# Router tail, threshold search and first expert lists of a GNN and mixture-of-experts kernel, rebuilt

## The reference

```python
x = x + _L1_gnn_ref(_layernorm(x), src, dst, ...)
# _L1_ffn_ref, on _layernorm(x):
capacity = max(1, int(Sz * CAP_FACTOR / E) + 1)          # 1250 * 2 / 8 + 1 = 313
scores = softmax(einsum('bsd,ed->bse', x, router_w))     # 8 experts
gate_vals, sel_idx = top_k(scores_t, capacity)           # 313 tokens for each expert
tokens = x[b_idx, sel_idx]
h = gelu(einsum('becd,edh->bech', tokens, w1) + b1)
y = einsum('bech,ehd->becd', h, w2) + b2
out = zeros_like(x).at[b_idx, sel_idx].add(y * gate_vals[..., None])
```

## Time and profile before

| | |
|---|---|
| median of 3 runs | 1624.05 us (1623.88 to 1624.58) |
| profiled execution | 1622.14 us, its span 1620.5 us |
| PE busy | 1487.8 us, 92% |
| DVE busy | 926.6 us, 57% |
| ACT / POOL busy | 592.5 / 351.0 us |
| mean granted TensorE clock | 0.963 of full |

### The profile page before, as it was taken

One profiled execution on the slowest core, in us unless ns is written; L12 is line 12 of the kernel. 1 busy time (PEld: TensorE's weight loads), 2 busy tenths in 40 slices (PEclk: granted clock), 3 DMA queues, 4 the chain that ended last, 5 costly groups with the idle time before them and its releaser, 6 DMA issues.

```text
span 1620.5 us, 30075 instructions
## 1 busy us (share of the span) xinstructions
PE 1487.8 (92%) x9025; PEld 801.8 (49%) x9025; DVE 926.6 (57%) x2130; ACT 592.5 (37%) x814; POOL 351.0 (22%) x300
## 2 busy tenths in 40 slices
PE   7887899999999999989999999999999728999996
PEld 5443454545455454434454444444545426667664
DVE  7886888686978887451432232223275565566542
ACT  4686647373535544220112220001122204465541
POOL 3222211202201110360800003500023201432232
PEclk9898899999999999999999999999999857999998
DMA  6000000000352433331301113420133335778753
GB/s 247 21 27 14 8 27 26 13 13 26 98 169 94 155 130 115 133 116 66 117 0 36 42 52 117 155 91 1 53 125 122 116 125 169 211 215 247 218 143 48
DMA packets 55682, 158.13 MB, mean 98 GB/s; under 512 B 6980, under 2 KB 8467, under 8 KB 55608
## 3 DMA queue, kind: packets, MB, share of 16 engines
q1 hardware_dynamic: 43704, 115.57, 19.9%
q0 software_dynamic: 11904, 41.62, 10.3%
HBM read 115.39 MB, written 41.78 MB: 97 GB/s over the span
## 4 chain that ended last, share of the span: by engine, by line
PE 72%; DVE 12%; issue 10%; ACT 3%; POOL 1%; DVEq 1%; DMA 1%; ACTq 0%; SPq 0%; POOLq 0%
PE ps L1219 25%; PE ps L1290 11%; PE ps L1414 8%; PE ps L1398 7%; PE ps L1130 3%; PE ps L1131 3%; PE ps L1132 3%; PE ps L1054 2%; PE ps L584 2%; PE ps L1386 1%; PE ps L1084 1%; DVE hm L1827 1%; DVE bstat L538 1%; ACT th L1484 1%; PE ps L1369 1%
## 5 line engine op out<-in xcount | busy, mean ns | idle before, releaser
L1219 PE MATMUL ps<-wa,tb 128*128 128x512 f16 x960 | 210.1, 379 | 3.7 <-DVEq L2176 1.6
L1290 PE MATMUL ps<-adj,nm 128*128 128x512 f16 (+1 forms) x960 | 178.6, 345 | 2.9 <-DVEq L2158 1.6
L1130 PE MATMUL ps<-gp,hop 128*128 (+1 forms) x400 | 152.8, 382 | 7.2 <-issue 3.7
L1131 PE MATMUL ps<-gp,hop 128*128 (+1 forms) x400 | 152.6, 382 | 0.0
L1132 PE MATMUL ps<-gp,hop 128*128 (+1 forms) x400 | 152.6, 382 | 0.0
L1219 PEld LDWEIGHTS ps<-wa,tb 128*128 (+1 forms) x960 | 92.9, 98 | 113.3 <-issue 4.3
L1290 PEld LDWEIGHTS ps<-adj,nm 128*128 x960 | 93.4, 97 | 88.5 <-issue 4.1
L1414 PE MATMUL ps<-wa,hT 128*105 128x512 f16 x576 | 126.8, 379 | 1.7 <-issue 1.7
L1591 ACT ACTIVATE tb<-cx 128x512 f32 (+1 forms) x48 | 26.8, 559 | 268.4 <-DVE cx L2148 268.4
L1219 PE MATMUL ps<-wb,hop 128*128 128x512 f16 x480 | 108.8, 388 | 0.0
L1398 PE MATMUL ps<-tkT,wb 128*128 128x315 f16 x768 | 107.2, 301 | 1.1 <-ACT tkT L1640 1.1
(11 more groups left out here) (361 smaller groups left out, 2372.1 us busy)
## 6 DMA issues: line engine op xcount, KB each, us to landing
w_st<-in_ew SPq DMA_DIRECT2D x16, 2048.0 KB, 10.5
self_d<-cr SPq DMA_DIRECT2D x20, 512.0 KB, 2.9
cr<-self_d SPq DMA_DIRECT2D x20, 512.0 KB, 4.3
stage<-in_wn POOLq DMA_DIRECT2D x16, 512.0 KB, 4.0
x_d<-cr SPq DMA_DIRECT2D x10, 512.0 KB, 4.5
cx<-x_d SPq DMA_DIRECT2D x10, 512.0 KB, 4.6
cr<-x_d SPq DMA_DIRECT2D x10, 512.0 KB, 4.3
out<-cr SPq DMA_DIRECT2D x10, 512.0 KB, 2.7
```

Of the source, the lines that this page charges most:

```text
L1130: pe.matmul(acc, wh, gh, start=(s_ == 0), stop=False, skip_group_check=True)
L1131: pe.matmul(acc, wh, gl, start=False, stop=False, skip_group_check=True)
L1219: ins = pe.matmul(ps[:, b + c, :], lhs(part, k), w[:, w_, k, c * 512:(c + 1) * 512], start=(k == 0 and part == 0 and w_ == 0), stop=(last ...
L1290: ins = pe.matmul(ps[:, 6 + j, 0:w_], nm[:, part, s_, bass.ds(f * P, P)], adj[:, s_, CC * c:CC * c + w_], start=(s_ == 0 and part == 0), s ...
```

## The change

`chained` takes a `tail`: the loop stops one turn earlier, and the last tiles are written out on each engine. There TensorE runs route(3, 1) before the transposes of tile 8, and route(4, 0) right behind them; ScalarE copies both parts of tile 8; the low part of tile 9 is made on VectorE, not on GpSimd; tile 9's three router products add up in one PSUM region, the maximum and the exponential read it there, and the mask of the padding rows (`live`) is folded into the last two operations.

In the search the ten rounds are unrolled on VectorE and TensorE. The number of cuts found is summed as integer powers of two straight into new bits (`found`), the next cuts are `base | found`, and `base` is made while TensorE counts. The compare is two instructions of five tiles each, and TensorE starts with the first. Constants are written early, in `first_low`.

For experts 0 and 1 TensorE waits for each one-hot tile by itself (tile outside, chunk inside). `s_idx` is signalled by the operation that writes `idx`. Each gathered chunk has its own semaphore, and TensorE waits for one chunk at a time, for all eight experts.

```diff
+def chained(loop, steps, tail, per=0, early=None):
...
-    with loop(1, NT // 2, per) as r:
+    with loop(1, NT // 2 - 1, per) as r:
         at(r, 0), at(r, 1)
-    at(NT // 2, 0, NT), at(NT // 2, 1, NT + 1)
+    at(NT // 2 - 1, 0)
+    tail()
...
-            with g.Fori(0, NT // 2) as r:
+            def full_d(i, j):
+                t = 2 * i + j
+                g.wait_ge(D_.aff, D_.r + t + 1)
+                g.sem_inc(s_tick, 1)
+                g.wait_ge(D_.lo, D_.m + t)
+                g.sem_inc(s_tick, 1)
+                g.tensor_scalar(cy[:, 0, :], cr[:, j, :], lnv[:, 1, j:j + 1], lnv[:, 2, j:j + 1],
+                                ALU.mult, ALU.add).then_inc(D_.y, 1)
+
...
+                g.wait_ge(D_.y, D_.n + 2 * i + j + 1)
+                g.sem_inc(s_tick, 1)
+                ln_low(g, D_, i, j, cy, dyh[:, j, 0, :], dyh[:, j, 1, :])
+
+            with g.Fori(0, NT // 2 - 1) as r:
...
-
-            g.wait_ge(s_live, 1)
+                    full_d(r, j), low_d(r, j)
+            full_d(NT // 2 - 1, 0), low_d(NT // 2 - 1, 0), full_d(NT // 2 - 1, 1)
...
+                if isinstance(t, int) and t == NT - 1:
+                    for k in range(KT):
+                        for n, (part, w_) in enumerate(((0, 0), (0, 1), (1, 0))):
+                            ins = pe.matmul(ps[:, 6 + j, 0:8], dyT[:, j, part, k, :], rws[:, k, 8 * w_:8 * w_ + 8],
+                                            start=(k == 0 and n == 0), stop=(k == KT - 1 and n == 2))
+                    ins.then_inc(D_.mm, 1)
...
+            def tail():
+                last = NT // 2 - 1
+                neighbours(1, last, 1), route(last - 1, 1)
+                turn_d(last, 0), route(last, 0)
+                turn_d(last, 1), route(last, 1)
+
...
-            with pe.Fori(0, BITS // STEP) as b:
-                pe.wait_ge(s_cm, b + 1)
+            for b in range(BITS // STEP):
                 for t in range(NT):
+                    if t % 5 == 0:
+                        pe.wait_ge(s_cm, 2 * b + t // 5 + 1)
                     ins = pe.matmul(ps[0:TP, 6, 0:CUTS * NE], ones16[0:TP, 0:TP], at_least[:, t].rearrange("p m n -> p (m n)"),
                                     start=(t == 0), stop=(t == NT - 1))
                 ins.then_inc(s_cnt, 1)
...
+                if isinstance(e, int) and e < 2:
+                    for t in range(NT):
+                        pe.wait_ge(s_sel0, NT * e + t + 1)
+                        for c in range(3):
+                            ins = pe.matmul(ps[0:SLOT, 0, 4 * c:4 * c + 4], selm[:, t, c * SLOT:(c + 1) * SLOT], tokg[:, t, e, :],
+                                            start=(t == 0 and c == 0), stop=(t == NT - 1), skip_group_check=True)
+                    ins.then_inc(s_lst, 1)
+                    return
...
-                pe.wait_ge(s_gx[j], 48 * (i + 1))
                 for c in range(3):
+                    pe.wait_ge(s_gx[j][c], 16 * (i + 1))
...
+            def tail():
+                last = NT // 2 - 1
+                evac_d(last, 0), evac_d(last, 0, 1)
+                ln_d(last, 1)
+                route(last - 1, 1), route(last, 0)
+                evac_d(last, 1), route(last, 1)
+
             chained(lambda a_, b_, _: s.Fori(a_, b_), [
...
+            def logits(i, j):
+                t = 2 * i + j
+                v.wait_ge(D_.mm, t + 1)
+                if isinstance(t, int) and t == NT - 1:
...
+                    link(v.tensor_reduce(col(j, 16), ps[0:TP, 6 + j, 0:8], AX_X, ALU.max))
+                else:
+                    link(v.tensor_copy(rtmp[:, j, 0:8], ps[0:TP, 6 + j, 8:16]))
+                    link(v.tensor_tensor(rtmp[:, j, 8:16], ps[0:TP, 6 + j, 0:8], rtmp[:, j, 0:8], ALU.add))
...
+            def scores(i, j):
+                t = 2 * i + j
+                v.wait_ge(s_dex, t + 1)
...
+                if isinstance(t, int) and t == NT - 1:
+                    link(v.tensor_scalar(col(j, 20), col(j, 19), live[:, 0:1], None, ALU.mult))
+                    v.tensor_scalar(sc[:, t, :], rtmp[:, j, 24:32], col(j, 20), live[:, 1:2], ALU.mult, ALU.add).then_inc(s_sc, 1)
+                else:
+                    v.tensor_scalar(tile_of(sc, t), rtmp[:, j, 24:32], col(j, 19), None, ALU.mult).then_inc(s_sc, 1)
...
+            def tail():
+                last = NT // 2 - 1
+                out_c(last, 1), stats_d(last, 1)
+                logits(last - 1, 1), logits(last, 0)
+                v.wait_ge(D_.y, D_.n + NT)
+                ln_low(v, D_, last, 1, cy, dyh[:, 1, 0, :], dyh[:, 1, 1, :])
+                scores(last - 1, 1), scores(last, 0)
+                evac_d(last, 1), route(last, 1)
+
+            chained(step.loop, [(out_c, 0), (stats_d, 0), (evac_d, 1), (route, 2)], tail, 2 * (1 + LINKS + 3), early=first_low)
 
...
+            found = thr[:, 1, :]
+            for b in range(BITS // STEP):
+                shift = BITS - STEP * (b + 1)
+                if b:
+                    link(v.tensor_tensor(cuts[:], base[:], per_cut(found), ALU.bitwise_or))
+                now = cuts if b else bits
+                for h in range(2):
+                    v.tensor_tensor(at_least[:, 5 * h:5 * h + 5], sc[:, 5 * h:5 * h + 5].unsqueeze(2).to_broadcast([TP, 5, CUTS, NE]),
+                                    now[:].bitcast(F32).unsqueeze(1).to_broadcast([TP, 5, CUTS, NE]), ALU.is_ge).then_inc(s_cm, 1)
+                if b < BITS // STEP - 1:
+                    if b:
+                        link(v.tensor_tensor(thr[:, 0, :], thr[:, 0, :], found, ALU.bitwise_or))
...
+                    v.wait_ge(s_cm, 2 * b + 2)
+                    link(v.tensor_scalar(bits[:], bits[:], 0.5 ** STEP, None, ALU.mult))
+                    link(v.tensor_tensor(base[:], per_cut(thr[:, 0, :]), bits[:], ALU.bitwise_or))
+                else:
+                    link(v.tensor_tensor(thr[:, 0, :], thr[:, 0, :], found, ALU.bitwise_or))
                 v.wait_ge(s_cnt, b + 1)
-                link(v.tensor_scalar(over[:], counts, float(CAP), None, ALU.is_ge))
-                link(v.tensor_reduce(nd[:, 0, :], over[:].rearrange("p m n -> p n m"), AX_X, ALU.add))
-                link(v.tensor_tensor(thr[:, 1, :], nd[:, 0, :], low_bit[:], ALU.mult))
-                link(v.tensor_tensor(thr[:, 0, :], thr[:, 0, :], thr[:, 1, :], ALU.bitwise_or))
+                link(v.tensor_scalar(over[:], counts, float(CAP), float(1 << shift), ALU.is_ge, ALU.mult))
+                with nc.allow_low_precision(reason="at most seven equal powers of two: exact as integers"):
+                    link(v.tensor_reduce(found, over[:].rearrange("p m n -> p n m"), AX_X, ALU.add))
+            link(v.tensor_tensor(thr[:, 0, :], thr[:, 0, :], found, ALU.bitwise_or))
...
+                    if isinstance(e, int) and e < 2:
+                        ins.then_inc(s_sel0, 1)
+                if not (isinstance(e, int) and e < 2):
+                    ins.then_inc(s_sel, 1)
...
+                v.tensor_tensor(idx[:, j, :], lst[:, j, :, 0], pads[:], ALU.add).then_inc(s_idx, 1)
...
-                v.sem_inc(s_idx, 1)
...
```

89 lines of the change are left out of this document (35 added, 54 removed).

## The result

| | median of the runs, us | ratio to before, 95% interval |
|---|---|---|
| before, in the same job | 1624.32 (1623.88 to 1625.63, 4 runs) | |
| after | 1609.96 (1607.34 to 1611.39, 4 runs) | 0.9909 [0.9893, 0.9924] |
| after, unedited, in a later job | 1607.27 (1605.83 to 1609.04, 4 runs) | 0.9894 [0.9879, 0.9908] |

The change saves 14.4 us in the first job and 16.9 in the later one, where before had a median of 1624.18; 15.7 was forecast. The profiled execution of after took 1611.06 us, its span 1609.4.

A forecast was written before the change was run, and what follows sets the result against it. In the search no engine is full; a serial chain from router tail to gathers delays the expert stage. 2.7 + 7.8 + 2.1 + 0.5 + 2.9 - 0.3 = 15.7 us; 1624.05 - 15.7 = 1608.4 us, range 1605.5 to 1611.8.

The forecast's parts named there:

- Tail: Router's last tiles: reordering, VectorE's subtraction and the shorter softmax start the first compare 2.7 us earlier, bounds 1.9 to 3.7.
- Search: Ten search rounds: 2.23 us per round in place of 3.02, gaining 7.8 us, bounds 5.4 to 8.6.
- the ring with its slower price: Second rival, search: each half compare held until the previous ends, round 2.5 us, saving 5.4, total 1610.8; chance 0.10.
- the slower case: Fourth rival: the unrolled search's instructions arrive late, 1.9 us or more lost per round, 1627.3 or more; chance 0.02.
- Lists: First expert's list: TensorE starts behind the first one-hot tile and trails, gaining 2.1 us, bounds 1.6 to 2.2.
- index: `s_idx` rises at an earlier operation, without a separate signal instruction: 0.5 us gained, between 0.4 and 0.9.
- Gathers: First expert's chunks: two are transposed before the third lands, gaining 2.9 us, at least 1.4.
- the third rival: Gathers: chunks land together or the landing comes 1.5 us later because expert 1's gathers share engines, 1609.8 to 1611.3; chance 0.10.
- Extra waits: Expert stage: two more TensorE waits for each of seven turns lose 0.3 us, between nothing and 0.7.
- a sign of being wrong: Expert stage, first matmul to end: growing by more than 1 us would show the prediction wrong.
- The first rival: TensorE's clock: full clock may return 3 us later beside the experts' work, costing 1.5 us, total 1609.9; chance 0.07.

The follow-up runs named there:

- after_again: The changed kernel, unedited, run again in a later job: 1607.27 us, ratio 0.9894.
- old_search: The changed kernel with the looped search of before put back, one compare and one signal per round: 1617.22 us, ratio 0.9958.
- old_tail_order: The changed kernel with the old order of the last router tiles and GpSimd's subtraction back, the last softmax still fused: 1610.81 us.
- one_compare: The changed kernel with one compare of 560 results per search round in place of two of 280: 1611.67 us, ratio 0.9925.
- second_gathers_held: The changed kernel with expert 1's gathers held on GpSimd until expert 0's third has landed: 1607.75 us, ratio 0.9895.
- gathers_together: The changed kernel with TensorE waiting for all three gathers of an expert ahead of its first transpose: 1609.89 us, ratio 0.9909.
- gathers_together_again: The changed kernel with all three gathers awaited together, run a second time in a later job: 1611.60 us, ratio 0.9927.
- fill_gathers: The changed kernel with ten added TensorE matmuls on constants around the second list and behind each chunk's transposes: 1607.74 us, ratio 0.9893.

## Why the prediction was right, point by point

**Tail, 2.7 forecast, 2.55 measured.** Each step came within 0.15: 0.92 us from the copy's end to VectorE (0.95 forecast), 0.45 to the exponential (0.5), 1.27 from there to the compare (1.25). The subtraction was timed right in its length (1.22). What was missed is small: VectorE came to it 0.5 us behind `cy`, where 0.3 was worked out.

**Search, 7.8 forecast, 7.87 measured.** The rounds, the first mark and the sum are right, and the ring with its slower price (2.5 us per round) is excluded. So is the slower case: the longest of the rounds takes 2.31 us, all behind it 2.18 or 2.19. The overlap that the row of before showed holds for the halves too: `thr` starts at 1303.33, while the second half runs until 1303.42. By the Trainium skill's page "VectorE: DVE Perf Modes", section "The DRAIN you can't avoid", it would have waited for that end, and there the measurement disagrees. The same section adds that an operation that isn't held starts earlier, which agrees; the prediction had left that sentence out. One sentence of this part is wrong: "VectorE is late, not the count: the halves gain nothing by themselves". The count's end was put at +1.29 and came at +1.27, but `over` follows it only at +1.39, a hand-over that the sum left out; the two limits are equal, and without the halves the count is late by 0.16 us per round (2.34 - 2.18). The halves gain 1.5 us.

**Lists 2.1, index 0.5; measured 1.93 and 0.52.** TensorE trails the one-hot tiles as described, ending 1.06 behind the last of them, where 0.9 was expected.

**Gathers, 2.9 forecast, 2.05 measured:** this is the term of the sum that was mis-sized. Its mechanism stands: three pieces, the third behind its landing. The size missed what the third rival named, in part. Before, the third chunk had landed 8.56 us behind the first gather's issue (1340.59 + 5.8 - 1337.83); after it landed 9.37 behind (1330.95 + 6.5 - 1328.08). That is 0.8 of the 0.85 us that are missing: 0.1 is the third gather's later issue, 0.7 its landing, which holding the next expert's gathers brought back to 5.8.

**Extra waits, -0.3 forecast.** The expert stage grew by 0.70, but not by the waits. In the second profile of after it grew by 1.02, which is past the 1 us that the prediction had named as a sign of being wrong; its clock came back 6.0 us behind the first expert matmul. The half clock that is left behind the first expert matmul explains it, in each kernel that doesn't keep TensorE warm through the search. Half of that stretch, taken off the stage, leaves 266.3 to 266.8 everywhere:

| kernel | first expert matmul | clock full at | ffn to end | less half the low stretch |
|---|---|---|---|---|
| before | 1351.96 | 1356.16 | 268.54 | 266.44 |
| after | 1340.16 | 1345.96 | 269.24 | 266.34 |
| after_again | 1337.84 | 1343.88 | 269.56 | 266.54 |
| old_search | 1348.87 | 1352.32 | 268.13 | 266.40 |
| old_tail_order | 1340.03 | 1344.12 | 268.47 | 266.42 |
| one_compare | 1339.80 | 1344.80 | 268.90 | 266.40 |
| second_gathers_held | 1339.49 | 1342.40 | 268.21 | 266.75 |
| gathers_together | 1344.54 | 1343.44 | 266.66 | 266.66 |
| gathers_together_again | 1342.30 | 1345.64 | 268.10 | 266.43 |
| fill_gathers | 1339.59 | 1338.80 | 266.51 | 266.51 |

Before and after differ by 0.1 there, less than the rows among themselves, so fourteen waits more cost nothing that can be seen. The first rival came true in part: the clock returned 5.8 us behind the first expert matmul, not 4.2, and cost 0.8 of the 1.5 that it was priced at.

The forecast leant against this rival on a rule of the Trainium skill, page "TensorE: Matmul & The Clock Gate", section "PE-mode transpose", by which transposes don't count as busy. In `gathers_together` TensorE did nothing but transposes from 1339.09 until the full clock came at 1343.44, and nothing at all in the 6.5 us ahead of them. So there the measurement speaks against the rule, and tying the clock to the first expert matmul was no safe argument. The second profile of that program, where the clock came 3.3 us behind that matmul, does not contradict the rule.

The clock is also where part of the gain on the gathers went. With the chunks awaited together 14.6 us pass to the first expert matmul, chunk by chunk 11.8 to 12.5, mean 12.2; but the clock comes back 13.5 and 17.9 us after the first gather with the chunks together and 15.3 to 18.5 chunk by chunk (after, after_again, old_search, old_tail_order, one_compare). So part of TensorE's earlier start is spent at half rate. From the first gather to the end it is 281.24 and 282.70 us with the chunks together, and 279.96 to 282.01, mean 281.0, chunk by chunk. About 1 us of 2.4 stays, and with two profiles on one side even that is not settled.

**Range and time.** 14.4 and 16.9 us saved lie on both sides of the forecast, but by the milestones both profiles of after are below it (14.4 and 13.7). That the first job's medians give the same 14.4 as its milestones is in part luck, as the spans of the profiled executions, 11.1 apart, show. As far as the two profiles show, what separates these two jobs is not in the changed part: from the last neighbour matmul to the end the two profiles of the same kernel differ by 0.67 us (325.54 and 326.21), and up to it by 2.67 the other way. The prediction spoke of no such spread; its range covered it by other reasons.

## What to carry to other kernels

In a ring of two engines work out both ways round to the point where they meet, the hand-over included: when they tie, each fix alone is worth next to nothing, and both together are worth what the table of four shows. Work that starts earlier while the clock is half counts half. So add to each wait removed ahead of a dense stage what it does to the moment the clock returns, and compare from a milestone, not from the span's start, when the unchanged part ahead moves by more than the effect. A transfer that is held back for the sake of another landed later itself here: look at who needs it.
